# Graph network of four layers on one core: moved loads and checks, a wider ring for one gather, and half of one scaling on ScalarE

## The reference

```python
x1 = _ln(x + [(1+eps)*x + segment_sum(relu(x[src] + edge_attr_48), dst)])
x2 = _ln(x1 + relu(h @ W1.T + b1))      # h: mean-like sum over dst of x1[src] / sqrt(out_deg[src]) / sqrt(in_deg[dst]);
                                        # h = x1 where a node has no incoming edge
x3 = _ln(x2 + relu(agg @ W2.T + b2))    # agg: sum over src of normed x2[dst]
x4 = _ln(x3 + layernorm(x3 + sum over src of gate*x3[dst]*cw*node_vec[dst] / tot) * gamma + beta))
# gate = silu(edge_attr_40 @ W.T + b) @ W.T + b + a factor that depends on the two node types
```

## Time and profile before

| what | value |
|---|---|
| time, median of 3 runs | 2563.16 us (2560.93 to 2564.61) |
| profiled execution: its time, its span | 2565.39 us, 2563.4 us |
| DVE busy | 1932.9 us, 75% of the span |
| POOL busy | 1781.0 us, 69% |
| ACT / PE / PE weight loads busy | 618.8 / 556.7 / 471.7 us |
| chain that ended last | DVE 47%, POOL 20%, issue 9%, PE 8%, DMA 8%, ACT 7% |
| granted TensorE clock, mean | 0.561 |
| moved by DMA | 276.19 MB |

### The profile page before, as it was taken

The page is one execution under the profiler, slowest core; times in us unless marked ns, Lnnn a source line. Parts: engine busy times, 40 slices in busy tenths (PEclk is TensorE's granted clock), DMA queues, the critical chain, the costliest instruction groups (busy, mean ns, idle before and its releaser), DMA issues.

```text
span 2563.4 us, 12772 instructions
## 1 busy us (share of the span) xinstructions
PE 556.7 (22%) x2848; PEld 471.7 (18%) x2848; DVE 1932.9 (75%) x2740; ACT 618.8 (24%) x1106; POOL 1781.0 (69%) x1768
## 2 busy tenths in 40 slices
PE   3800000006787375532310000006200000000000
PEld 1300000006777254432310000006200000000000
DVE  5889999997888675553484099984699999988881
ACT  4910022213443221111110023231112222321110
POOL 4777777775777767737776676767777774637776
PEclk9955555556666576755555555555555555555555
DMA  4169589823445333298009644452232222210000
GB/s 137 21 230 329 156 322 330 299 69 111 158 147 168 104 72 69 51 54 56 17 13 67 87 131 142 124 160 63 50 84 79 82 79 83 65 37 17 17 16 15
DMA packets 158466, 276.19 MB, mean 108 GB/s; under 512 B 88601, under 2 KB 113507, under 8 KB 158259
## 3 DMA queue, kind: packets, MB, share of 16 engines
q1 hardware_dynamic: 96675, 206.39, 28.6%
q0 software_dynamic: 56448, 44.23, 10.3%
q10 hardware_dynamic: 5264, 24.74, 2.7%
HBM read 142.41 MB, written 138.17 MB: 109 GB/s over the span
## 4 chain that ended last, share of the span: by engine, by line
DVE 47%; POOL 20%; issue 9%; PE 8%; DMA 8%; ACT 7%; SPq 1%; ACTq 0%; DVEq 0%; POOLq 0%
POOL out L520 7%; POOL ring L465 7%; POOL x_table L520 6%; DVE PS L1343 5%; PE PS L897 5%; DVE du L1346 5%; DVE var L1352 4%; DVE do L1363 3%; DMA x_table<-sumb,put 3%; PE PS L883 3%; DVE sumb L1271 3%; DMA din<-in_xaux 2%; DMA din<-x_table 2%; ACT GX L661 2%; DVE du L1577 2%
## 5 line engine op out<-in xcount | busy, mean ns | idle before, releaser
L605 ACT ACTIVATE sq<-du 128x1344 f32<-128x1344 f32 x129 | 169.2, 1321 | 541.5 <-DVE du L1346 518.5
L520 POOL DMA_INDIRECT x_table<-sumb,put x196 | 212.5, 1084 | 114.1 <-issue 58.2
L508 POOL DMA_INDIRECT ring<-h_by_src,zs x196 | 204.0, 1041 | 98.8 <-issue 58.5
L478 POOL DMA_INDIRECT XD<-in_xaux,srcI x196 | 201.0, 1025 | 86.3 <-issue 59.1
L520 POOL DMA_INDIRECT out<-sumb,put x196 | 192.6, 982 | 96.5 <-issue 61.8
L465 POOL DMA_INDIRECT ring<-x_with_degree,srcI x196 | 203.7, 1039 | 80.4 <-issue 60.6
L520 POOL DMA_INDIRECT x_with_degree<-sumb,put x196 | 193.8, 989 | 86.7 <-issue 57.3
L465 POOL DMA_INDIRECT ring<-edge_records,dstI x196 | 185.9, 949 | 91.4 <-issue 57.9
L478 POOL DMA_INDIRECT XD<-x_table,srcI x196 | 196.3, 1002 | 59.7 <-issue 59.7
L478 POOL DMA_INDIRECT XD<-xa_table,dstI x196 | 191.1, 975 | 59.7 <-issue 59.4
L866 PE MATMUL PS<-ident,tail 128*49 128x128 f32 x10 | 4.5, 447 | 911.1 <-DVEq L1045 911.1
(11 more groups left out here) (271 smaller groups left out, 2489.7 us busy)
## 6 DMA issues: line engine op xcount, KB each, us to landing
din<-in_xaux SPq DMA_DIRECT2D x56, 728.0 KB, 5.0
xa_table<-din SPq DMA_DIRECT2D x28, 728.0 KB
x_table<-GX SPq DMA_DIRECT2D x28, 686.0 KB
x_with_degree<-GX SPq DMA_DIRECT2D x28, 686.0 KB
din<-x_table SPq DMA_DIRECT2D x28, 686.0 KB
x_table<-do SPq DMA_DIRECT2D x28, 672.0 KB
din<-x_table SPq DMA_DIRECT2D x28, 672.0 KB
out<-do SPq DMA_DIRECT2D x28, 672.0 KB
```

The costliest lines, as they stand in the source:

```text
L478: pool.indirect_dma_start(XD[:, t, 0:w], None, table, bass.IndirectOffsetOnAxis(ap=of[:, t:t + 1], axis=0)).then_inc(rows[c].sem, rows[c]. ...
L508: pool.indirect_dma_start(ring4[:, c % 4, t, :], None, H2, bass.IndirectOffsetOnAxis(ap=of[:, c * H + t:c * H + t + 1], axis=0), bounds_ch ...
L520: pool.indirect_dma_start(table, bass.IndirectOffsetOnAxis(ap=put[:, c * H + t:c * H + t + 1], axis=0), rows_of[:, h, t, :], None, bounds_ ...
L605: nc.scalar.activation(sq[:, h, :, :], u, ACT.Square).then_inc(S["squared"], 1)
```

## The change

Five things are changed.

- **Early check.** DVE looks at dst first, as soon as dst, shifted dst and `ident` are in (`look` now counts three loads); constants and `init` come behind it. The other 24 constants are issued by ACT.
- **Edge loads.** src has a semaphore of its own (`src_in`); POOL's first gather and the histogram wait for it alone, and the block `order`/`writers` stands behind the histogram.
- **Table pass.** Four buffers (`xab`: both halves of `din`, and space in `du` and `sq`); a load waits for the store two blocks before it, and is issued behind the next block's store.
- **Dense pass 1.** DVE multiplies the reciprocals of half 1 by the factor (28 numbers) and scales half 0 only. ACT scales half 1 in 28 instructions, one for each of a partition's rows, and copies its degrees. The stores of the two halves wait for different semaphores (`out0`, `out1`). DVE centers half 1 of the next pair only when ACT is through (`scaled1`).
- **Gather and staging.** The ring for Y1 has four slots of 49 columns (`gather_x1`). ACT stages chunk 2 behind step i = 4 of the rows, chunk 3 behind i = 6, and chunk n+4 at the start of pair n, n = 0 to 9.

```diff
-AT_START = {0: 2, 1: 3, 2: 4, 3: 5, 4: 6, 5: 7, 8: 11}
-AT_END = {5: 8, 6: 9, 7: 10, 8: 12, 9: 13}
+AT_START = {n: n + 4 for n in range(10)}
...
+        xab = [din[:, h, :] for h in range(2)] + [
+            t.rearrange("p h c d -> p (h c d)")[:, 0:R * XW] for t in (du[:, :, :, :], sq[:, :, :, :])]
...
+        ring4y = ring[:, :, :, :].rearrange("p h c w -> p (h c w)")[:, 0:4 * H * YW].rearrange(
+            "p (h c d) -> p h c d", h=4, d=YW)
...
+            for k in range(4):
+                xa_load(k)
+            for k in range(DBLK):
+                xa_store(k)
+                if 2 <= k < DBLK - 2:
+                    sp.wait_ge(xst[(k - 2) % 4].sem, xst[(k - 2) % 4].now())
+                    xa_load(k + 2)
...
-                sp.wait_ge(out_ready.sem, out_ready.up())
+                sp.wait_ge(out_ready[h].sem, out_ready[h].up())
...
+            def gather_x1(of):
+                filled = views("y_fill0", "y_fill1", "y_fill2", "y_fill3")
+                for c in range(CE // H):
+                    if c >= 4:
+                        pool.wait_ge(S["ring_free"], c - 3)
+                    for t in range(H):
+                        pool.indirect_dma_start(
+                            ring4y[:, c % 4, t, :], None, Y1,
+                            bass.IndirectOffsetOnAxis(ap=of[:, c * H + t:c * H + t + 1], axis=0)
+                                ).then_inc(filled[c % 4].sem, filled[c % 4].add())
...
-            pool.wait_ge(edges.sem, edges.up(5))
+            pool.wait_ge(S["src_in"], 16)
             gather_in_place(A["xaux"], XW, srcI)
             pool.wait_ge(S["xa_done"], 1)
+            pool.wait_ge(edges.sem, edges.up(4))
             gather_in_place(XA, XW, dstI, xs_free)
...
+            for n in range(DBLK // 2):
                 norm(pair, c2s[:, 0:1])
+                act.wait_ge(S["scale1"], n + 1)
+                if n:
+                    act.wait_ge(S["st1"], 32 * n)
+                for c in range(R):
+                    nc.scalar.activation(do1[:, 1, c, 0:D], du[:, 1, c, :], ACT.Copy, scale=srs[:, 1, c:c + 1]
+                                         ).then_inc(own.sem, own.add())
+                nc.scalar.activation(do1[:, 1, :, D], deg[:, (2 * n + 1) * R:(2 * n + 2) * R], ACT.Copy
+                                     ).then_inc(own.sem, own.add())
+                act.wait_ge(own.sem, own.now())
+                act.sem_inc(S["out1"], 1)
+                act.sem_inc(S["scaled1"], 1)
...
-                if i == 0:
-                    to_stage1(0)
-                    to_stage1(1)
+                for c in {0: (0, 1), 4: (2,), 6: (3,)}.get(i, ()):
+                    to_stage1(c)
...
+                    if h == 1 and scaled:
+                        dve.wait_ge(S["scaled1"], scaled)
                     V.scalar_tensor_tensor(u, along(mean[:, h, :]), -1.0 / D, x, ALU.mult, ALU.add
                                            ).then_inc(S["centered"], 1)
...
+                if scaled is not None:
+                    V.tensor_scalar(srs[:, 1, :], inverse[:, 1, :], factor, None, ALU.mult).then_inc(S["scale1"], 1)
+                    units = units[:1]
...
+            dve.wait_ge(S["scaled1"], DBLK // 2)
...
-            dve.wait_ge(S["edges"], 16 * 5)
-            V.tensor_copy(key[:, :], dstI[:, :]).then_inc(own.sem, own.add())
-            V.tensor_copy(keyn[:, :], t0[:, :].bitcast(I32)).then_inc(own.sem, own.add())
-            one(V.tensor_copy(nv[:, :], cnt[:, :].bitcast(I32)))
-            order(key[:, :], keyn[:, :], nv[:, :])
-            flipped(restT, suf[:, 0:1])
-            writers(key[:, :])
-
+            dve.wait_ge(S["src_in"], 16)
             one(V.tensor_copy(colf, srcI[:, :]))
...
             dve.sem_inc(S["deg_done"], 1)
 
+            dve.wait_ge(S["edges"], 16 * 4)
+            V.tensor_copy(key[:, :], dstI[:, :]).then_inc(own.sem, own.add())
+            V.tensor_copy(keyn[:, :], t0[:, :].bitcast(I32)).then_inc(own.sem, own.add())
+            one(V.tensor_copy(nv[:, :], cnt[:, :].bitcast(I32)))
+            order(key[:, :], keyn[:, :], nv[:, :])
+            flipped(restT, suf[:, 0:1])
+            writers(key[:, :])
```

More of the change, by code:

```diff
@@ L480, in gather_in_place @@
                                 ).then_inc(rows[c].sem, rows[c].add())
-            def gather(table, w, of, first=0, **skip):
-                for c in range(first, CE // H):
-                    gather_turn(table, w, of, c, **skip)
-                for h in range(2):
-                    pool.wait_ge(fill[h].sem, fill[h].now())
+            def gather_x1(of):
[8 more added lines that the diff above has]
+                                ).then_inc(filled[c % 4].sem, filled[c % 4].add())
             rb_st, (ring_read,) = views("rb_st0", "rb_st1"), views("ring_read")
@@ L1338, in _, with norm @@
             mean, inverse, shift = muP, srsP, carryP
-            def norm(units, factor=None, free=False, stores=False, keep=None):
+            def norm(units, factor=None, free=False, stores=False, scaled=None):
                 for h, x, u, out in units:
```

179 lines of the change are left out of this document (84 added, 95 removed).

## The result

| kernel | median | runs | range |
|---|---|---|---|
| before | 2563.74 us | 6 | 2560.69 to 2569.95 |
| changed | 2552.56 us | 6 | 2547.16 to 2556.36 |

The ratio is 0.9949 (95% interval 0.9936 to 0.9962): 10 to 16 us faster. The forecast was 34 us (2529, range 2518 to 2544): the sign is right, the size wrong by more than 20 us. The profiled execution of the changed kernel took 2556.36 us, with a span of 2554.5.

A forecast was written before the change was run, and what follows sets the result against it. The prediction took POOL's indirect DMAs and the waits for their rows, the chain up to message 13, as the bound. Four slots gave 38.3 us, less 4 in dense pass 2: 2563.2 - 34.3 = 2529 us, range 2518 to 2544.

The forecast's parts named there:

- Part 2, the constants: Kernel start: constants on ACT's queue last used at about 15.6 us; DVE 3.4 us earlier after 1 us off for ea48.
- DVE's lead: Kernel start: DVE's sum loop starts 4.4 us earlier, 3.4 us after 1 us is taken off for ea48.
- The rival that named the constants: Before the scatter: ACT pieces of 0.3 us, or constants 5 to 10 us late; 2536 to 2543 us; chance 0.17.
- Part 2, the rest: Kernel start: flag at about 7.6 us, POOL's first gather about 15.2 us earlier, first histogram piece at 27.2.
- Part 1: Gather of x1: with four slots chunk 6, not chunk 4, goes out on message 2; minus 38.3 us.
- Its condition: Gather of x1: six chunks must precede message 2, so the gather has to start by about 797 instead of 821.42.
- Part 3, the table pass: Table pass: stays hidden by POOL's first gather, zero gain; as the bound a 6 us wait of POOL.
- Dense pass 1: Pair time 13.8 us instead of 14.1, 4 us gained, minus 2.9 for ACT's last half; in sum 1 us gained.
- the piece: Dense pass 1: each of ACT's 28 scaling instructions takes 0.24 us, 6.7 us together; bounds 0.15 and 0.41.
- Part 4, the stall of ACT: Staging of chunk 4: ACT stands 7 us for POOL; dense pass 2 with message 2 runs about 4 us later.
- Sum: Whole kernel: 38.3 - 4 = 34.3 us off, giving 2529 us; chance of 28 to 38 us off 0.52.

The follow-up runs named there:

- held: Changed kernel, but SP sends ea48 and the four table loads only when DVE is about to start the histogram: 2510.56 us, ratio 0.9844 to the kernel before.

## Why the prediction was wrong, by its steps

- **Part 2, the constants: this step failed.** The prediction has them "last used at about 15.6 if nothing disturbs them", and takes 1 us off for ea48, within a bound of 10. They came 16.3 us later. The bound itself was wrong in kind: it counted ea48's bytes at 327 GB/s, while the two queues take turns by packets, so that hundreds of tiny packets wait for the bulk to end. It also left out that the table loads now go out in the same 4 us. DVE's lead was not +3.4 but -11.1: dense pass 1 starts at 323.69 where it was at 312.62. The rival that named the constants went to 10 us and was still too mild; the sentence from the Trainium skill that spoke against the step (Trainium Kernel Development and Optimization, Key Constraints: the queues share 16 engines) pointed the right way, though by it the constants would only have gained nothing, and I set it aside because no row showed the two kinds of load together. The runs that hold the bulk show the step by itself: constants used at 16.5 to 16.7, and 17 us of time.
- **Part 2, the rest: right.** Flag at 7.3 (7.6), first gather 16.5 us earlier (15.2), and with the loads held the histogram at 27.8 (27.2).
- **Part 1, right**, with 37.0 us on the first chip (193.6 less 156.6, forecast 38.3), 31.0 and 34.6 on chip B, from message 2 to message 13 40.7 (changed) and 38.4 (held) less than before on chip C, and DVE's waits at 21.9 (23). Its condition was met only because message 2 was late: the gather started at 808.7.
- **Part 3, the table pass: right**, hidden. **Dense pass 1: the piece was priced right, the sum had the wrong sign.** In the groups of the changed kernel:

```profile
L691 ACT ACTIVATE GX<-du,srs 128x48 f32<-128x48 f32 x392 | 89.8, 321 | 9.6 <-DVE srs L1379 9.6
```

392 pieces in 89.8 us are 6.4 us for 28 (forecast 6.7; by the Trainium skill's price, ScalarE: Activation LUTs, What ACT_TABLE_LOAD costs, 6.3 as an estimate). A pair takes 13.89 us (13 pairs from 323.69 to 504.22), before 14.06: 2 us won where I had 4, since DVE now waits 1.4 to 2.7 us a pair for its loads (0.2 to 1.1 before):

```profile
490.67 3.02 DVE L1362 TENSOR_REDUCE PS<-din 128x28 f32<-128x1344 f32 x2 [1.99 <-DMA din<-in_xaux]
...
504.22 3.02 DVE L1362 TENSOR_REDUCE PS<-din 128x28 f32<-128x1344 f32 x2 [1.43 <-DMA din<-in_xaux]
...
521.18 1.55 DVE L1354 TENSOR_TENSOR sub<-pre,PS 128x1344 f32<-128x1344 f32 x1 [4.99 <-ACTq L697]
```

The wait for ACT's last half is there (4.99), and from the last pair's start to the first stage copy it costs 3.4 us (2.9 forecast). Two readings of the rows were off without weight: the first gather ended at 287.7 in the kernel before, not about 285, and POOL has one more wait there, 3.5 us before chunk 3 of the gather of x1.
- **Part 4, the stall of ACT, didn't appear.** In the changed kernel DVE was too late for it. With the loads held until the histogram the other conditions of the forecast are met (chunk 2 copied at 570.8, forecast 570.0), and still ACT copied chunk 4 without a wait:

```profile
592.58 0.76 ACT L706 ACTIVATE sumb<-XD 128x672 f32<-128x672 f32 x1
...
599.58 0.97 POOL L514 DMA_INDIRECT x_with_degree<-sumb,put  x1 [0.30 <-issue]
```

The second row is POOL's eighth DMA of chunk 3, where the prediction had the half of the stage come free (its end forecast at 597.7). It was free 7 us before that. The release stands behind that DMA in the program and waits for chunk 2 to land, whose last DMA starts at 589.37. In the kernel before on chip C, the one wait of ACT for POOL in this stretch ends at 764.42, when the chunk whose half it needs can just have landed (its last DMA starts at 762.11) and POOL's rows show one DMA of the next chunk, not eight. So the half comes free with the landing, ahead of POOL's rows; why its queue is ahead of them I didn't test. Message 2 stood at 905.0, 0.5 us later than before, where the forecast had it 4 us later although all ahead of it would be 4 earlier. That the sum still came near is two errors against each other: the stall of ACT isn't there, and the rows of layer 1 were staged 0.3 us earlier than before (529.2 against 529.5), not 4.4, since dense pass 1 took 2.1 us longer.
- **Sum.** By the steps: 37 won by the slots, 19 lost in front of message 2 (11 from the start, 1 in dense pass 1, 1 in the copies that now stand ahead of dense pass 2, 6 in its pairs: from the first evacuation to message 0 they take 266.6 us, 261.5 before, and 258.7 to 269.7 in other traces with the same code there), 9 lost behind message 13, which I put down to clock and landings of one execution. That is 9, as the two traces have it; the medians have 11. Why the pairs of dense pass 2 differ so much between executions is open.

## What to carry to other kernels

Before a small load is moved to a queue of its own, look at what the other queues send at that moment, and count packets, not bytes: here hundreds of tiny ones beside large ones ended with the large ones or just behind them. Put the bulk behind them, in the same queue or behind a wait, and let it go as late as its reader allows; here one wait was worth more than every other part but the slots. A deeper buffer is worth only as many chunks as its producer can have out by then, so its price hangs on when the producer starts.

## What was new about the hardware

- Two hardware queues and POOL's took turns packet by packet: 39, 39 and 38 packets in 4 us, where the constants' queue moved 633 without the bulk, and the time from the last constant's issue to its use went from 3.2 us in the kernel before to 18.8.
- The stand behind the branch on the flag was 3.9 to 5.0 us, and 6.6 to 6.9 in the four runs that let 3 to 7.8 MB go 1.3 to 6 us ahead of it; one packet on an instruction queue came 2.0 to 3.3 us into the stand in the one case and 4.5 to 5.3 in the other.
- ACT took a half of the stage 7 us before the row of the POOL DMA behind which its release is programmed (592.58 and 599.58 us).
- The same kernel's time differs between chips by 0.5% (before: 2550 to 2564 us). The scatter of x2 took 276 to 280 us in the fourteen traces of chips B, C and D, and 293 to 296 in the two first ones, whose chip is not on record.
